# 47 matmuls of a zero tile ahead of the first product of a joint-classifier kernel

## The chip, the cores and the metric

The kernel runs on one NeuronCore of a Trainium2 chip. The metric is the device time of one execution in microseconds (us). The engines are TensorE (PE, with its weight loads as PEld), VectorE (DVE), ScalarE (ACT), GpSimd (POOL) and SyncE (SP), each with its own instruction stream; they meet at semaphores.

## The reference

Each of 512 rows has 64 logits, four variables of 16. Four softmaxes are joined by outer products to 65,536 values a row. The labels sum them to class counts, these are divided by the sum over rows, and the ratios are applied to the same joint values.

```python
splits = np.cumsum((16, 16, 16, 16))[:-1]
variables = [jax.nn.softmax(p, axis=-1) for p in jnp.split(logits, splits, axis=-1)]
joint = variables[0]
for v in variables[1:]:
    joint = jnp.einsum('b...,ba->b...a', joint, v)
flat = joint.reshape(B, -1)                              # 512 x 65536
num_y_joint = jnp.einsum('bj,by->yj', flat, y_true)      # y_true is 512 x 100
num_joint = jnp.sum(flat, axis=0)
prob_y_joint = jnp.clip(jnp.maximum(num_y_joint, 1e-6) / jnp.maximum(num_joint, 1e-6), 0.0, 1.0)
probs = jnp.einsum('yj,bj->by', prob_y_joint, flat)
```

## The kernel before

The joint value is split in two factors. `p` is (variable 1) x (variable 2) x (variable 3), cut into 32 tiles of 128 joint indices by 512 rows; `q` is (variable 0) x (labels and a column of ones), in four groups of four values of variable 0, 4 x 101 = 404 columns each. The 512 rows lie as 128 partitions by KC = 4 chunks. Products need more than fp16, so p and q are split in high and low fp16 parts, and each product is three matmuls: high by high, high by low, low by high.

There are 4 groups x 32 tiles = 128 steps. A step has a *count* on TensorE (12 matmuls of 404 columns into a PSUM bank `numbers0` to `numbers3`, lines 366 to 373), a *ratio* on VectorE (five instructions, `make_ratios`, lines 276 to 293), and a *join* on TensorE (12 matmuls of 400 columns into `joined0` to `joined3`, lines 384 to 390). TensorE runs four counts ahead of the joins, one bank a slot; joins also need the transposed p (`pt_hi`, `pt_lo`), which SyncE makes by DMA transposes from `p_hi` and `p_lo` in the first group. After a group's last join ScalarE copies the joined banks out, and GpSimd folds them into `acc`; for the last group VectorE does this itself, in 16 adds (line 354), before the store.

The order is written out by hand, engine by engine, with semaphores. The start is this. SyncE loads the logits. VectorE subtracts the maximum, ScalarE takes exp, VectorE makes `v1s`, the first half of `p23` (line 235, semaphore `p23_made`), the sums and `v0n` (line 304, `v0n_made`), the first half of `qf` (line 243), the second half of `p23` and of `qf`. ScalarE makes `p_hi` of tile 0 (four activations, line 187), the first half of `q_hi` (line 195), `p_hi` of tile 1, the second half of `q_hi`, and then `p_hi` of tiles 2 and 3, four activations of 128x256 together, and so on in a loop. VectorE makes `q_lo` (line 249) and `p_lo` (line 270) behind them.

TensorE does nothing until p_hi's tile 0 and q_hi's first half are there. Its first four counts are split up by hand so that each matmul stands as early as its operands come (lines 404 to 435): two products of tile 0 and two of tile 1 with the first half of `q_hi`, four with the second half, four with the first half of `q_lo`, then, behind a wait for `p_hi_made` 4, eight products of tiles 2 and 3, then four more with `q_lo` and the `p_lo` products. From then on joins and counts alternate.

GpSimd's only work at the start is the memset of the ones column of `labels` and of `acc`. `SLOTS` is 4, `LANES` 128.

Of the kernel before, what the change touches and what calls it, by code (L numbers as in the profile page):

```python
# [25 lines left out]
FP16 = mybir.dt.float16  # L26
# [5 lines left out]
def joint_classifier(nc: bass.Bass, logits: bass.AP, y_true: bass.AP, probs: bass.AP):  # L32
    ROWS, WIDTH = logits.shape
    CLASSES = y_true.shape[1]
    LANES = 128
# [20 lines left out]
    with ctx:  # L56
        def sb(name, shape, dt):
            return ctx.enter_context(nc.sbuf_tensor(name, shape, dt))

        def pb(name, shape, dt):  # L60
            return ctx.enter_context(nc.psum_tensor(name, shape, dt))

        def sem(name):
            return ctx.enter_context(nc.semaphore(name))

        SLOTS = 4
        TURN_SEMS = 4

        x = sb("x", [LANES, KC * NV, S], FP32)
# [3 lines left out]
        v0f = sb("v0f", [LANES, KC, S], FP32)  # L73
        v1s = sb("v1s", [LANES, KC, S], FP32)
        labels = sb("labels", [LANES, KC, CW], FP32)
        p23 = sb("p23", [LANES, KC, 2 * HALF], FP32)

        p_hi = sb("p_hi", [LANES, TILES * TW], FP16)
# [6 lines left out]

        den = sb("den", [LANES, SLOTS, AG], FP32)
        inv = sb("inv", [LANES, SLOTS, AG], FP32)
        ratio = sb("ratio", [LANES, SLOTS, PW], FP32)
        r_hi = sb("r_hi", [LANES, SLOTS, PW], FP16)
        r_lo = sb("r_lo", [LANES, SLOTS, PW], FP16)  # L90

# [3 lines left out]

        numbers = [pb(f"numbers{i}", [LANES, 512], FP32) for i in range(SLOTS)]
        joined = [pb(f"joined{i}", [LANES, 512], FP32) for i in range(KC)]
# [6 lines left out]
        shifted = sem("shifted")  # L104
        exps = sem("exps")
        v1s_made = sem("v1s_made")
        v0n_made = sem("v0n_made")
        p23_made = sem("p23_made")
        q_made = sem("q_made")
# [4 lines left out]
        p_ready = sem("p_ready")  # L114
        pt_landed = [sem(f"pt_landed{j}") for j in range(TURN_SEMS)]
        numbers_ready = sem("numbers_ready")
# [16 lines left out]
        @block.sync  # L133
        def _(sp):
            sp.dma_start(x[:, :, :], logits.rearrange("(p k) (v s) -> p (k v) s", k=KC, s=S)).then_inc(logits_in, 16)

            def turn(out, src, i):
                return sp.dma_start_transpose(
                    out[:, i * 2 * TW:(i + 1) * 2 * TW].rearrange("p (c b) -> p c b", b=LANES),
                    src[:, i * 2 * TW:(i + 1) * 2 * TW])  # L140

            for i in range(S):
                landed = pt_landed[i % TURN_SEMS]
                if i >= TURN_SEMS:
                    sp.wait_ge(landed, i // TURN_SEMS * 32)
                sp.wait_ge(p_hi_made, 2 * i + 2)
                turn(pt_hi, p_hi, i).then_inc(landed, 16)
                sp.wait_ge(p_ready, 2 * i + 2)
                turn(pt_lo, p_lo, i).then_inc(landed, 16)
            sp.wait_ge(added, KC * AG)  # L150
            sp.dma_start(probs.rearrange("(p k) y -> p k y", k=KC), acc[:, :, :]).then_inc(stored, 16)
            sp.wait_ge(stored, 16)

        @block.gpsimd
        def _(pool):
            pool.memset(labels[:, :, CLASSES:CW], 1.0).then_inc(ones_set, 1)
            pool.memset(acc[:, :, :], 0.0).then_inc(acc_set, 1)
            pool.wait_ge(p_ready, TILES)
            pool.tensor_scalar(v0f[:, :, :], v0n[:, :, :], 1.0 / UP ** 3, None, ALU.mult).then_inc(v0f_made, 1)
            pool.wait_ge(v0f_made, 1)  # L160
            pool.wait_ge(acc_set, 1)
            with pool.Fori(1, GROUPS) as g:
                pool.wait_ge(left_made, g * KC)
                pool.tensor_tensor(part[:, :, :, :], left[:, :, :, :],  # L164
                                   v0f[:, :, bass.ds((g - 1) * AG, AG)].unsqueeze(3).broadcast_to([LANES, KC, AG, CLASSES]),
                                   ALU.mult).then_inc(sum_chain, 1)
                pool.wait_ge(sum_chain, 3 * g - 2)
                pool.tensor_tensor(part[:, :, 0:2, :], part[:, :, 0:2, :], part[:, :, 2:4, :],
                                   ALU.add).then_inc(sum_chain, 1)
                pool.wait_ge(sum_chain, 3 * g - 1)  # L170
                pool.tensor_tensor(part[:, :, 0, :], part[:, :, 0, :], part[:, :, 1, :], ALU.add).then_inc(sum_chain, 1)
                pool.wait_ge(sum_chain, 3 * g)
                pool.tensor_tensor(acc[:, :, :], acc[:, :, :], part[:, :, 0, :], ALU.add).then_inc(summed, 1)

                pool.wait_ge(summed, g)
# [183 lines left out]
        def _(pe):  # L359
# [24 lines left out]
            def join(g, tile, slot, first=False, final=False):  # L384

                pe.wait_ge(ratios_ready, g * TILES + tile + 1)
                for k in range(KC):
                    if first and g:
                        pe.wait_ge(left_made, (g - 1) * KC + (k + 1))
                    join_chunk(tile, slot, k, first, final)  # L390
# [7 lines left out]
            def first_lo_hi(tile):  # L398
# [2 lines left out]
                                     start=False, stop=(k == KC - 1))  # L401
                last.then_inc(numbers_ready, 1)

            pe.wait_ge(p_hi_made, 1)
            pe.wait_ge(q_hi_made, 1)
            for k in range(KC // 2):
# [30 lines left out]
            for tile in range(TILES - SLOTS):  # L437
                if tile % 2 == 0:
                    pe.wait_ge(pt_landed[tile // 2 % TURN_SEMS], (tile // 2 // TURN_SEMS + 1) * 32)
                join(0, tile, tile % SLOTS, first=(tile == 0))  # L440
# [4 lines left out]
            for g in range(GROUPS):  # L445
# [8 lines left out]
                if g < GROUPS - 1:  # L454
                    pe.wait_ge(q_ready, 2 + (g + 1) * KC)
                    for j in range(SLOTS):
                        tile = TILES - SLOTS + j
                        if g == 0 and j % 2 == 0:
                            pe.wait_ge(pt_landed[tile // 2 % TURN_SEMS], (tile // 2 // TURN_SEMS + 1) * 32)
                        join(g, tile, j, final=(j == SLOTS - 1))  # L460
# [33 lines left out]
```

## Time and profile before

| | us |
|---|---|
| Median of 3 runs | 540.55 |
| Lowest and highest of them | 540.05, 541.52 |
| The profiled execution | 540.03 |
| Its span, first to last instruction | 537.8 |
| PE busy | 524.5 (98%) |
| DVE busy | 294.3 (55%) |
| ACT busy | 41.5 (8%) |
| First matmul starts | 8.24 |

The rows below come from the profiled execution. Times are microseconds from the start of its span. In a timeline row the first number is the start and the second the duration, and square brackets tell how long the engine was idle before and which instruction released it. A matmul's duration reaches over the start of the next one, as matmuls are pipelined; the pace of TensorE is the distance between two starts. PEclk is the granted TensorE clock as a share of 2.4 GHz as the profiler recorded it.

### The profile page before, as it was taken

To read this page: it belongs to the slowest core of one execution; us is meant where nothing else is said; L and a number is where in the kernel's file an instruction comes from. 1 tells how busy PE (TensorE), PEld (TensorE's weight loads), DVE (VectorE), ACT (ScalarE), POOL (GpSimd) and SP (SyncE) were. 2 spreads that over 40 slices of the span, in tenths; PEclk is the share of its full clock that TensorE was granted. 3 is DMA by queue.
4 is the path that set the end of the run, shared out by engine and by line. 5 is a ranking of instruction groups with operands and counts; after the bars stand their busy time and mean duration, and the time that the engine had idled before them with its cause. 6 is when DMAs were issued, how large, how long until landed. Compare 5 with 4: busy or idle time off the path is not lost.

```text
span 537.8 us, 8613 instructions
## 1 busy us (share of the span) xinstructions
PE 524.5 (98%) x3072; PEld 299.5 (56%) x3072; DVE 294.3 (55%) x757; ACT 41.5 (8%) x96; POOL 22.5 (4%) x19
## 2 busy tenths in 40 slices
PE   3999999999999999999999999999999999999996
PEld 1555555555555555555555555555555555555553
DVE  7887667654575444444467444444446444444445
ACT  6950000000110000000020000000001000000000
POOL 0000000000050000000022000000005000000000
PEclk9999999999999999999999999999999999999999
DMA  1744243340000000000000000000000000000000
GB/s 45 141 95 66 53 78 60 59 60 1 0 1 1 1 0 0 0 0 0 0 1 1 0 0 0 1 0 0 0 0 1 0 1 0 0 0 0 0 0 15
DMA packets 34624, 9.17 MB, mean 17 GB/s; under 512 B 34352, under 2 KB 34608, under 8 KB 34608
## 3 DMA queue, kind: packets, MB, share of 16 engines
q1 hardware_dynamic: 34080, 8.73, 8.8%
q8 instruction: 13, 0.21, 0.2%
q10 hardware_dynamic: 528, 0.20, 0.1%
q14 instruction: 3, 0.02, 0.0%
HBM read 0.34 MB, written 0.20 MB: 1 GB/s over the span
## 4 chain that ended last, share of the span: by engine, by line
PE 97%; DVE 2%; ACT 0%; DMA 0%; issue 0%; ACTq 0%; DVEq 0%
PE joined L378 16%; PE joined L379 16%; PE joined L380 16%; PE numbers L370 16%; PE numbers L372 16%; PE numbers L371 16%; DVE acc L354 1%; PE numbers L393 1%; PE numbers L396 1%; PE numbers L400 1%; DMA x<-in_r_logits_dram 0%; ACT p_hi L187 0%; DVE qf L243 0%; ACT q_hi L195 0%; DVE p L235 0%
## 5 line engine op out<-in xcount | busy, mean ns | idle before, releaser
L379 PE MATMUL joined<-r_lo,pt_hi 128*128 128x400 f16 x512 | 170.4, 333 | 0.0
L380 PE MATMUL joined<-r_hi,pt_lo 128*128 128x400 f16 x512 | 170.4, 333 | 0.0
L378 PE MATMUL joined<-r_hi,pt_hi 128*128 128x400 f16 x512 | 170.3, 333 | 0.0
L370 PE MATMUL numbers<-q_hi,p_hi 128*128 128x404 f16 x496 | 166.5, 336 | 0.0
L372 PE MATMUL numbers<-q_hi,p_lo 128*128 128x404 f16 x496 | 165.5, 334 | 0.0
L371 PE MATMUL numbers<-q_lo,p_hi 128*128 128x404 f16 x496 | 165.4, 333 | 0.0
L280 DVE TENSOR_SCALAR den<-numbers 128x4 f32<-128x4 f32 x128 | 20.7, 162 | 215.9 <-PE numbers L372 215.0
L292 DVE SCALAR_TENSOR_TENSOR r_lo<-ratio,r_hi 128x400 f16<-128x400 f32 x128 | 78.4, 612 | 4.4
L285 DVE SCALAR_TENSOR_TENSOR ratio<-numbers,inv 128x400 f32<-128x400 f32 x128 | 73.5, 574 | 4.4
L379 PEld LDWEIGHTS joined<-r_lo,pt_hi 128*128 (+1 forms) x512 | 50.0, 98 | 36.9
L378 PEld LDWEIGHTS joined<-r_hi,pt_hi 128*128 (+1 forms) x512 | 49.8, 97 | 37.0
L380 PEld LDWEIGHTS joined<-r_hi,pt_lo 128*128 (+1 forms) x512 | 50.0, 98 | 36.6
L371 PEld LDWEIGHTS numbers<-q_lo,p_hi 128*128 (+1 forms) x496 | 48.7, 98 | 36.2
L372 PEld LDWEIGHTS numbers<-q_hi,p_lo 128*128 (+1 forms) x496 | 48.0, 97 | 36.9
L370 PEld LDWEIGHTS numbers<-q_hi,p_hi 128*128 (+1 forms) x496 | 48.3, 97 | 36.1
L290 DVE TENSOR_SCALAR r_hi<-ratio 128x400 f16<-128x400 f32 x128 | 48.9, 382 | 4.4
L221 ACT ACTIVATE left<-joined 128x400 f32<-128x400 f32 x12 | 5.9, 503 | 317.8 <-PE joined L380 317.7
L187 ACT ACTIVATE p_hi<-p,v1s 128x256 f32 (+1 forms) x68 | 26.6, 480 | 0.9 <-DVE p L235 0.9
L270 DVE SCALAR_TENSOR_TENSOR p_lo<-p,v1s,p_hi 128x256 f16<-128x256 f32 x64 | 26.6, 480 | 0.0
L283 DVE RECIPROCAL inv<-den 128x4 f32<-128x4 f32 x128 | 22.8, 178 | 4.4
L164 POOL TENSOR_TENSOR part<-left,v0f 128x1600 f32<-128x1600 f32 x3 | 8.6, 2862 | 277.7 <-ACT left L221 277.7
L393 PE MATMUL numbers<-q_hi,p_hi 128*128 128x404 f16 x16 | 4.7, 432 | 8.5 <-ACT q_hi L195 8.2
(31 smaller groups left out, 62.5 us busy)
## 6 DMA issues: line engine op xcount, KB each, us to landing
pt_hi<-p_hi SPq DMA_TRANSPOSE x16, 3.1
pt_lo<-p_lo SPq DMA_TRANSPOSE x16, 3.2
labels<-in_r_y_true_dram ACTq DMA_DIRECT2D x1, 200.0 KB, 2.8
out_dram<-acc SPq DMA_DIRECT2D x1, 200.0 KB, 1.9
x<-in_r_logits_dram SPq DMA_DIRECT2D x1, 128.0 KB, 2.2
```

What stands on the lines that cost most here:

```text
L187: last = act.activation(o[:, h0:h1, k, :], p23[:, k, h0 * HALF:h1 * HALF].rearrange("p (h n) -> p h n", n=HALF), ACT.Copy, scale=v1s[:, k, ...
L270: last = dve.scalar_tensor_tensor(lo[:, :, k, :], p23[:, k, :].rearrange("p (h n) -> p h n", n=HALF), v1s[:, k, bass.ds(i, 1)], hi[:, :, k ...
L283: dve.reciprocal(inv[:, slot, :], den[:, slot, :]).then_inc(inv_made, 1)
L285: dve.scalar_tensor_tensor(ratio[:, slot, :].rearrange("p (a y) -> p a y", a=AG), got[:, :, 0:CLASSES], STABLE, inv[:, slot, :].unsqueeze( ...
L290: dve.tensor_scalar(r_hi[:, slot, :], ratio[:, slot, :], UP, 0.0, ALU.min, ALU.max).then_inc(r_hi_made, 1)
L292: dve.scalar_tensor_tensor(r_lo[:, slot, :], ratio[:, slot, :], UP, r_hi[:, slot, :], ALU.min, ALU.subtract).then_inc(ratios_ready, 1)
L370: pe.matmul(out, p_at(p_hi, tile, k), q_at(q_hi, g, k), start=(k == 0), stop=False)
L371: pe.matmul(out, p_at(p_hi, tile, k), q_at(q_lo, g, k), start=False, stop=False)
L372: last = pe.matmul(out, p_at(p_lo, tile, k), q_at(q_hi, g, k), start=False, stop=(k == KC - 1))
L378: pe.matmul(out, p_at(pt_hi, tile, k), r_hi[:, slot, :], start=first, stop=False)
L379: pe.matmul(out, p_at(pt_hi, tile, k), r_lo[:, slot, :], start=False, stop=False)
L380: last = pe.matmul(out, p_at(pt_lo, tile, k), r_hi[:, slot, :], start=False, stop=final)
```

## The change

A tile `idle` of 128x256 fp16 is set to zero by GpSimd, ahead of its two other memsets. On TensorE, ahead of the first product, 47 matmuls are written out: the weights are the tile's first 128 columns, the moving operand all 256 of them, the output 256 columns of the PSUM bank `numbers0`. That bank is later started anew by the first product (`start=True`), so that nothing of the zeros is left. 22 of the 47 wait for the zero tile, nine for the first half of `p23`, and 16 for `v0n`. All else, the products' order and waits included, is as before; only line numbers move (393 is 398 in the changed kernel, 396 is 401).

```diff
+        IDLE_W = 256
+        IDLE_START, IDLE_EXPS, IDLE_V0 = 22, 9, 16
...
+        idle = sb("idle", [LANES, IDLE_W], FP16)
...
+        idle_set = sem("idle_set")
...
         def _(pool):
+            pool.memset(idle[:, :], 0.0).then_inc(idle_set, 1)
             pool.memset(labels[:, :, CLASSES:CW], 1.0).then_inc(ones_set, 1)
...
+            def idle_turns(n):
+                for _ in range(n):
+                    pe.matmul(numbers[0][:, 0:IDLE_W], idle[:, 0:LANES], idle[:, :], start=True, stop=True)
+
+            pe.wait_ge(idle_set, 1)
+            idle_turns(IDLE_START)
+            pe.wait_ge(p23_made, 1)
+            idle_turns(IDLE_EXPS)
+            pe.wait_ge(v0n_made, 1)
+            idle_turns(IDLE_V0)
+
             pe.wait_ge(p_hi_made, 1)
             pe.wait_ge(q_hi_made, 1)
```

TensorE's stream begins like this before the change (the first row is the block's entry):

```order
L358 UNCONDITIONAL_BRANCH [waits barrier_Pool_Activation_PE_DVE_SP_release]
L393 MATMUL numbers<-q_hi,p_hi 128x404 [waits q_hi_made,p_hi_made]
L393 MATMUL numbers<-q_hi,p_hi 128x404
L393 MATMUL numbers<-q_hi,p_hi 128x404 [waits p_hi_made]
L393 MATMUL numbers<-q_hi,p_hi 128x404
L393 MATMUL numbers<-q_hi,p_hi 128x404 [waits q_hi_made]
L393 MATMUL numbers<-q_hi,p_hi 128x404 x3
L396 MATMUL numbers<-q_lo,p_hi 128x404 [waits q_ready]
```

And like this after it:

```order
L363 UNCONDITIONAL_BRANCH [waits barrier_Pool_Activation_PE_DVE_SP_release]
L411 MATMUL numbers<-idle 128x256 [waits idle_set]
L411 MATMUL numbers<-idle 128x256 x21
L411 MATMUL numbers<-idle 128x256 [waits p23_made]
L411 MATMUL numbers<-idle 128x256 x8
L411 MATMUL numbers<-idle 128x256 [waits v0n_made]
L411 MATMUL numbers<-idle 128x256 x15
L398 MATMUL numbers<-q_hi,p_hi 128x404 [waits q_hi_made,p_hi_made]
L398 MATMUL numbers<-q_hi,p_hi 128x404
```

The first product now stands behind 47 matmuls and three more waits; from it on the rows are the same.

GpSimd's stream at the entry of its block, before:

```order
L154 UNCONDITIONAL_BRANCH [waits barrier_Pool_Activation_PE_DVE_SP_gather]
L156 MEMSET labels 128x4
L157 MEMSET acc 128x400
L159 ISA
L159 TENSOR_SCALAR v0f<-v0n 128x64 [waits p_ready]
```

and after:

```order
L158 UNCONDITIONAL_BRANCH [waits barrier_Pool_Activation_PE_DVE_SP_gather]
L160 MEMSET idle 128x256
L161 MEMSET labels 128x4
L162 MEMSET acc 128x400
L164 ISA
L164 TENSOR_SCALAR v0f<-v0n 128x64 [waits p_ready]
```

The zero tile's memset has gone in front of the two others, and nothing else has moved.

## Rows read from the trace of the kernel before

**Rows 1.** The page: busy time (share of the span), and the chain that ended last by engine.
```profile
PE 524.5 (98%) x3072; PEld 299.5 (56%) x3072; DVE 294.3 (55%) x757; ACT 41.5 (8%) x96; POOL 22.5 (4%) x19
PE 97%; DVE 2%; ACT 0%; DMA 0%; issue 0%; ACTq 0%; DVEq 0%
```

**Rows 2.** Windows, all engines: length, busy us (xinstructions), PEclk, DMA share, GB/s.
```profile
12.19:530.00 517.81, 517.81 (x3045) 296.65 (x3044) 281.27 (x726) 33.50 (x79) 21.88 (x13) 1.00 0.09 16
```

**Rows 3.** Timeline of PE, one row a matmul: start us, us, engine, line, operation [idle].
```profile
8.24 0.49 PE L393 MATMUL numbers<-q_hi,p_hi 128*128 128x404 f16 x1 [8.24 <-ACT q_hi L195]
9.31 0.52 PE L393 MATMUL numbers<-q_hi,p_hi 128*128 128x404 f16 x1 [0.25 <-ACT p_hi L187]
10.08 0.52 PE L393 MATMUL numbers<-q_hi,p_hi 128*128 128x404 f16 x1
10.39 0.54 PE L393 MATMUL numbers<-q_hi,p_hi 128*128 128x404 f16 x1
11.06 0.54 PE L393 MATMUL numbers<-q_hi,p_hi 128*128 128x404 f16 x1
11.40 0.44 PE L396 MATMUL numbers<-q_lo,p_hi 128*128 128x404 f16 x1
11.68 0.51 PE L396 MATMUL numbers<-q_lo,p_hi 128*128 128x404 f16 x2
12.02 0.34 PE L396 MATMUL numbers<-q_lo,p_hi 128*128 128x404 f16 x1
12.19 0.33 PE L393 MATMUL numbers<-q_hi,p_hi 128*128 128x404 f16 x1
```

**Rows 4.** Timeline of PE and its weight loads at the first join.
```profile
18.38 0.33 PE L378 MATMUL joined<-r_hi,pt_hi 128*128 128x400 f16 x1
18.38 0.10 PEld L379 LDWEIGHTS joined<-r_lo,pt_hi 128*128 128x128 f16 x1
18.54 0.33 PE L379 MATMUL joined<-r_lo,pt_hi 128*128 128x400 f16 x1
```

**Rows 5.** Windows of PE's first products and of the end; PE's last matmul in the timeline.
```profile
8.24:11.40 3.16, 2.91 (x8) 1.00 0.28 56
...
537.00:537.70 0.70, 0.00 (x0) 0.00 (x0) 0.00 (x0) 0.00 (x0) 0.00 (x0) 0.68 0.00 0
...
532.69 0.33 PE L380 MATMUL joined<-r_hi,pt_lo 128*128 128x400 f16 x1
```

**Rows 6.** Timeline of ACT: q_hi's second half and the last p_hi of tiles 2, 3.
```profile
9.17 0.86 ACT L195 ACTIVATE q_hi<-qf 128x808 f16<-128x808 f32 x1
11.13 0.49 ACT L187 ACTIVATE p_hi<-p,v1s 128x256 f32 x1
```

**Rows 7.** Timeline of DVE and SP to the first join; the page's transposes (median us to landing).
```profile
10.06 1.00 DVE L249 TENSOR_TENSOR q_lo<-qf,q_hi 128x808 f16<-128x808 f32 x1 [0.45 <-ACT q_hi L195]
13.74 0.48 DVE L270 SCALAR_TENSOR_TENSOR p_lo<-p,v1s,p_hi 128x256 f16<-128x256 f32 x1
15.14 0.16 DVE L280 TENSOR_SCALAR den<-numbers 128x4 f32<-128x4 f32 x1 [0.91 <-PE numbers L400]
16.56 0.58 DVE L292 SCALAR_TENSOR_TENSOR r_lo<-ratio,r_hi 128x400 f16<-128x400 f32 x1
12.67 1.23 SPq L138 DMA_TRANSPOSE pt_lo<-p_lo  x1
...
pt_lo<-p_lo SPq DMA_TRANSPOSE x16, 3.2
```

**Rows 8.** Timeline of POOL at the start.
```profile
0.71 0.10 POOL L156 MEMSET labels<- 128x4 f32 x1 [0.29 <-POOLq L482]
0.75 0.43 POOL L157 MEMSET acc<- 128x400 f32 x1
```

**Rows 9.** Timeline of DVE: the first half of p23 (p) and v0n.
```profile
4.38 0.68 DVE L235 TENSOR_TENSOR p<-x 128x512 f32<-128x512 f32 x1
5.92 0.23 DVE L304 SCALAR_TENSOR_TENSOR v0n<-x,whole 128x64 f32<-128x64 f32 x1
```

## The prediction

> **What bounds the kernel now.** I read the busy shares first: PE is busy 98% of a span of 537.8 us, and the chain that ended last is 97% PE [rows 1]. Then the windows: from 12.19 to 530.00 us PE is busy 517.81 of 517.81 us [rows 2], so whatever time PE gains or loses by 12.19 us is carried to its last matmul, and to the 16 adds on VectorE and the store behind it, which wait for that. What is before 12.19 us decides this change, since nothing behind it is edited.
>
> There the PE timeline, one matmul a row, has to be read by start-to-start distance [rows 3]. Products of 404 columns that wait for nothing start at 10.39, at 11.06 (the next but one) and at 11.40 us, 0.34 us a product: 404 columns in 0.337 us are 1.2 GHz. From 12.02 to 12.19 it is 0.17 us, which is 2.4 GHz, and it stays so (18.38 and 18.54 us, [rows 4]). The one after 11.40 starts at 11.68, an intermediate distance, so the clock rose near 11.6 us, about 3.4 us after the first matmul at 8.24. The granted-clock column prints 1.00 for 8.24 to 11.40 as well [rows 5]; it contradicts the distances, and I go by the distances. It does print the fall: 0.68 in 537.00 to 537.70, while the last matmul starts at 532.69 and lasts 0.33 [rows 5]. So PE kept the full clock through at least 3.9 us of idleness.
>
> **What a full clock at the first product is worth.** I walk PE's waits with 0.17 us a product. Products 1 and 2 start at 8.24, as before, for q_hi's first half. Products 3 and 4 wait for p_hi and start at 9.31. The next four wait for q_hi's second half (ACT 9.17 + 0.86 = 10.03) and start at 10.08 [rows 3, 6]; four products end their turn at 10.08 + 0.68 = 10.76, and four with q_lo at 11.44. Now PE meets a wait that the low clock had hidden: the eight products of tiles 2 and 3 wait for p_hi_made 4, the last of four activations, 11.13 + 0.49 = 11.62 [rows 6]. With the 0.05 us that stood between ACT's end and PE's start at 10.08, they start at 11.67 instead of 12.19. **Gain: 0.52 us.** The ten or so products at the low clock take 10 x 0.167 = 1.7 us more than at the full one, but most of that lies in PE's waits for ScalarE.
>
> What is late next? The products of q_lo's second half need 10.06 + 1.00 = 11.06; they would start at 13.04. The p_lo products of tiles 0 and 1 would start at 13.73 and need their p_lo, for which SyncE's transpose waits too; it is issued at 12.67. Those of tiles 2 and 3 would start at 16.48 and need 13.74 + 0.48 = 14.22 themselves. The first join would start at 18.38 - 0.52 = 17.86; the ratios it needs end at 16.56 + 0.58 = 17.14 and follow PE earlier, since VectorE stood idle 0.91 us before den (from 14.22 it could start), and that transpose, which the join needs, lands 3.2 us later, 15.9 [rows 7]. Nothing takes the 0.52 us back.
>
> **The idle matmuls, part by part.** *Start.* GpSimd's first memset in the block stands at 0.71, and 128x400 of fp32 takes 0.43 us [rows 8]; a 128x256 fp16 tile lies between 0.10 and 0.43, I take 0.3. So PE starts near 1.05 us (bounds 0.85 to 1.2). The labels' and acc's memsets move back by as much; the ones are first read behind v0n, at 6.15 us [rows 9], so this costs nothing. *One matmul.* No row has 256 columns with 128 rows of fp16; scaled from the rows it is 256/404 of 0.337 = 0.213 us at 1.2 GHz and of 0.170 = 0.108 us at 2.4 GHz. Its weight load takes 0.10 us and runs beside the matmul before it [rows 4], so the lower bound is 0.108 and the upper, if the load hides nothing, 0.21; the hidden load is what every row shows. *Clock.* If it rises 3.4 us after the first matmul, as before, that is at 4.4 us. Then 16 matmuls run low, six high, and batch one ends near 5.1; p23 is there at 4.38 + 0.68 = 5.06 [rows 9]. Batch two ends near 6.05, v0n comes at 5.92 + 0.23 = 6.15, and batch three, 16 x 0.108 = 1.7 us, ends at 7.9, before the first product's 8.24. The two small holes are far below the 3.9 us idleness that kept the clock up [rows 5].
>
> *If it rises later*, more of the 47 run low and the last ends later. With a rise at 8.0 us, 33 run low until 8.1, and the last ends at 8.1 + 14 x 0.108 = 9.6; the twelve products behind it, full speed, 2.04 us, then end at 11.65, just where ScalarE lets PE on anyway. So the gain of 0.52 us is whole for every rise up to 8.0 us, and it is used up (idle matmuls ending at 10.15, since 12.19 - 2.04 = 10.15) only by a rise near 9.1, some 8 us after the first matmul. Everything else on PE, in particular order and waits, stands as it was.
>
> **Span and medians.** The profiled execution took 540.03 us (span 537.8 and 2.2 around it). 540.03 - 0.52 = 539.51. Its time lies 0.52 under the median of 540.55, and the three timed runs spread over 1.47 us. A rise that comes later in some executions explains such a spread well, as each us of dense products at half clock costs up to half a us: 1.47 us would be 2.9 us later. If so, the changed kernel, whose clock may rise as late as 8.0 us without a loss (4.4 + 2.9 = 7.3), sheds this spread too, and its median is near 539.5. If the spread has another source (the input's DMA ahead of all work, for one), it stays, and the median is 540.55 - 0.52 = 540.03. The Trainium skill, TensorE: Matmul & The Clock Gate, section "What's actually happening", says that the point of the rise varies from run to run of one kernel. The one trace here can't show that; by the trace alone 540.03 would stand, by the page 539.5. I take 539.6, nearer the first, since the profiled run coincides with the fastest of the three, as it would if the rise had its earliest place there.
>
> **Rivals.**
> 1. *Spread stays*: gain only against the same execution, 540.0 us. For it: a clock record of one execution proves nothing on others. Against: a low clock is the only part of this kernel seen here that changes within an execution.
> 2. *Gain does not come*: the zero matmuls take longer than their columns, or the clock rises after 9.1 us. With 16 at the low clock until 4.4 us, the other 31 may take (10.15 - 4.4) / 31 = 0.185 us each before the gain is gone. If the 0.10 us load hid nowhere, they would take 0.31 us low and 0.21 high: 11 by 4.4 us, 36 more until 11.9, the twelve products until 13.9, which is 1.7 us late. That spans 540.0 to 542.3, and I give the middle of partly hidden loads, 540.3 to 540.9. Against: the load hides in every 0.17 us, and 0.098 still fits in 0.108.
> 3. *Slower*: matmuls of zeros do not raise the clock. All 47 at 0.213 take 10.0 us and end at 11.1; the first product moves from 8.24 to 11.1 and the clock rises 3.4 us later, at 14.5. Ten products at 0.337 and two at 0.17 end at 14.8 against 12.19: +2.6 us, 542.7 on the profiled execution, 543.2 on the median. It decides from an idle end of 10.15 on. For it: no row shows the clock with zero data. Against: both clock levels here stood with the same kind of data, so nothing ties the clock to data rather than to matmuls issued.
> 4. *The change does more*: over 1.6 us gained would need early waits on ScalarE or VectorE to go as well; none is touched.
>
> **How the numbers follow.** Clock up in time and spread shed (539.5): 0.50. Clock up, spread kept (540.0): 0.32. No gain (540.3 to 540.9): 0.11. Slower (542.7): 0.04. Faster than all this: 0.03, of which 0.02 beyond 0.3%. I predict 539.6; the range is 539.1 to 540.8: 0.4 under the likeliest case for what PE and DMA starts vary, and up over most of the no-gain case. 0.3% is 1.6 us, about what a measurement of this kernel can tell from no change: faster is under 538.9, slower over 542.2. That gives faster 0.02, same 0.94, slower 0.04.
>
> **What would show it.** In the profile after: idle matmuls start near 1.05 us at 0.21 us and change to 0.11 before 8.0 us; the last ends by 8.24 to 9.6; the first product is followed by the second 0.17 us later; the eight products of tiles 2 and 3 start at 11.67, released by ACT's p_hi; the first join at 17.86; span 537.3. Wrong, if products still stand 0.33 us apart, if the first product starts after 9.6, or if the eight products start near 12.19 or later; and the spread of the timed runs tells between rival 1 and the forecast: shed, it is under 0.7 us.

## The result, and the profile after

| | before | after |
|---|---|---|
| Median of 14 runs, us | 540.6 | 539.47 |
| Lowest and highest, us | 540.05, 541.52 | 539.37, 539.55 |
| Ratio of the mean times, 95% interval | | 0.9977 (0.9969 to 0.9985) |
| Profiled execution, us | 540.03 | 539.47 |
| Its span, us | 537.8 | 537.2 |

The change takes 1.1 us or 0.21% off the median, and the distance from the lowest to the highest run goes from 1.47 to 0.18 us. The profiled execution shows 0.6 us of it; the rest is that the execution profiled before was one of the fastest of its kernel.

The page of the kernel after, its busy shares and the chain by engine, which answers to [rows 1]:

```profile
PE 531.1 (99%) x3119; PEld 305.4 (57%) x3119; DVE 294.3 (55%) x757; ACT 41.5 (8%) x96; POOL 22.8 (4%) x20
PE 96%; DVE 2%; ACT 1%; DMA 0%; issue 0%; ACTq 0%; DVEq 0%
```

PE has 47 matmuls more (3119 against 3072) and 6.6 us more busy time in a span that is 0.6 us shorter. The time at stake is in the first 12 us. This is the timeline of PE there (start us, us, engine, line, operation, how many; in brackets the idle time before and its releaser), to be laid beside [rows 3]; lines 393, 396 and 400 of before are 398, 401 and 405 here:

```profile
1.08 7.94 PE L411 MATMUL numbers<-idle 128*128 128x256 f16 x47 [1.08 <-POOL idle L160]
8.86 0.90 PE L398 MATMUL numbers<-q_hi,p_hi 128*128 128x404 f16 x4
10.01 0.86 PE L398 MATMUL numbers<-q_hi,p_hi 128*128 128x404 f16 x4 [0.25 <-ACT q_hi L200]
10.71 0.85 PE L401 MATMUL numbers<-q_lo,p_hi 128*128 128x404 f16 x4
11.61 1.55 PE L398 MATMUL numbers<-q_hi,p_hi 128*128 128x404 f16 x8
12.99 0.85 PE L401 MATMUL numbers<-q_lo,p_hi 128*128 128x404 f16 x4
13.68 1.54 PE L405 MATMUL numbers<-q_hi,p_lo 128*128 128x404 f16 x8
...
17.81 0.33 PE L383 MATMUL joined<-r_hi,pt_hi 128*128 128x400 f16 x1
```

The idle matmuls run from 1.08 us to the first product at 8.86. The first four products stand 0.17 to 0.21 us apart, the next four start at 10.01 behind ScalarE, and the eight of tiles 2 and 3 start at 11.61, where they stood at 12.19. The first join is at 17.81 (18.38 before). The last matmul starts at 532.12 (532.69 before), and the distance from first join to last matmul is 514.31 us in both, so what is gained at the start arrives whole at the end. From 11.61 to 530 us PE has no idle time (window of PE: length, busy us, matmuls, PEclk, DMA share, GB/s):

```profile
11.61:530.00 518.39, 518.39 (x3047) 1.00 0.09 16
```

The pace of the idle matmuls is read from windows of PE: length, busy us, (matmuls that touch the window), PEclk, DMA share, GB/s. The clock column stays at 1.00 here as it did in [rows 5]:

```profile
5.00:6.00 1.00, 1.00 (x7) 1.00 0.00 0
6.00:6.50 0.50, 0.50 (x4) 1.00 0.00 0
6.50:7.00 0.50, 0.50 (x6) 1.00 0.00 0
7.00:8.00 1.00, 1.00 (x12) 1.00 0.00 0
```

Seven matmuls touch the us from 5 to 6, twelve the one from 7 to 8. The matmuls overlap, so these counts are two or so above the number of starts, but the change of pace lies near 6.5 us: 5.4 us after the first matmul, at 1.08, and before the first product.

What releases the two later groups of products is in ScalarE's timeline, which answers to [rows 6]:

```profile
9.09 0.86 ACT L200 ACTIVATE q_hi<-qf 128x808 f16<-128x808 f32 x1
```

```profile
11.06 0.49 ACT L192 ACTIVATE p_hi<-p,v1s 128x256 f32 x1
```

q_hi's second half ends at 9.95 and PE goes on at 10.01; the last p_hi of tile 3 ends at 11.55 and PE goes on at 11.61. In this execution the logits landed 0.08 us earlier than in the one before: VectorE's first reduce starts at 2.83 (2.91 before). Of the 0.58 us between 12.19 and 11.61, then, 0.08 are the input's and 0.50 the change's.

### The profile page after: what moved, and what is told of

Same layout as the page of the kernel before. It is cut to its first block, busy times and chain, and to the rows that moved or that the text cites. A ratio compares the mean times of both kernels' runs of the same rounds, so it can differ in the third digit from the quotient of the medians.

```text
span 537.2 us, 8708 instructions
## 1 busy us (share of the span) xinstructions
PE 531.1 (99%) x3119; PEld 305.4 (57%) x3119; DVE 294.3 (55%) x757; ACT 41.5 (8%) x96; POOL 22.8 (4%) x20
## 4 chain that ended last, share of the span: by engine, by line
PE 96%; DVE 2%; ACT 1%; DMA 0%; issue 0%; ACTq 0%; DVEq 0%
PE joined L383 16%; PE joined L385 16%; PE joined L384 16%; PE numbers L375 16%; PE numbers L376 16%; PE numbers L377 16%; DVE acc L359 1%; PE numbers L405 1%; DMA x<-in_r_logits_dram 0%; PE numbers L401 0%; ACT p_hi L192 0%; PE numbers L398 0%; ACT q_hi L200 0%; DVE qf L248 0%; DVE p L240 0%
## 5 line engine op out<-in xcount | busy, mean ns | idle before, releaser
L375 PE MATMUL numbers<-q_hi,p_hi 128*128 128x404 f16 x496 | 166.1, 335 | 0.0
L248 DVE TENSOR_TENSOR qf<-v0n,labels 128x404 f32<-128x404 f32 (+1 forms) x14 | 10.5, 753 | 0.0
```

What stands on the lines that cost most here:

```text
L375: pe.matmul(out, p_at(p_hi, tile, k), q_at(q_hi, g, k), start=(k == 0), stop=False)
```

## The experiments

All numbers are medians of 5 to 14 runs, with the lowest and the highest, in us. Each set had runs of the kernel before on the same chip beside it; their medians were 540.6 to 540.8, and they went from 539.74 to 541.52. A ratio is that of the mean times, to the kernel before of the same set.

| | idle matmuls | order of products | median | lowest, highest |
|---|---|---|---|---|
| the kernel before | none | as before | 540.6 | 540.05, 541.52 |
| the change | 22, 9, 16 | as before | 539.47 | 539.37, 539.55 |
| e1_one_each | 1, 1, 1 | as before | 540.67 | 540.27, 541.25 |
| e2_start_only | 22, 0, 0 | as before | 540.66 | 539.99, 541.47 |
| e3_ones | 22, 9, 16, of ones | as before | 539.46 | 539.37, 539.54 |
| e4_plus16 | 22, 9, 32 | as before | 539.63 | 539.39, 540.74 |
| e6_third_batch_only | 0, 0, 16 | as before | 539.86 | 539.38, 540.57 |
| e12_third_batch_4 | 22, 9, 4 | as before | 539.45 | 539.39, 539.56 |
| e13_no_third_batch | 22, 9, 0 | as before | 539.46 | 539.39, 540.87 |
| e7_order_no_idle | none | both edits | 540.81 | 540.05, 541.18 |
| e10_swap_and_idle | 22, 9, 16 | first edit | 539.46 | 539.40, 539.56 |
| e9_chunks_and_idle | 22, 9, 16 | second edit | 539.15 | 538.95, 539.21 |
| e8_order_and_idle | 22, 9, 16 | both edits | 538.58 | 538.41, 538.72 |
| e11_both_12 | 22, 9, 12 | both edits | 538.62 | 538.59, 538.73 |

### Is it the matmuls, or what comes with them? (e1_one_each)

```diff
-        IDLE_START, IDLE_EXPS, IDLE_V0 = 22, 9, 16
+        IDLE_START, IDLE_EXPS, IDLE_V0 = 1, 1, 1
```

> One zero matmul in each of the three batches instead of 22, 9 and 16; the tile, its memset and the three waits stay. Theory (the gain is the clock, raised by the 47): the gain and the narrow spread both go, median 540.4 to 540.8 us, spread of the runs over 1 us, products 0.34 us apart until 11 us or later. Rival (the gain comes from the layout, the memset, the waits or from TensorE's instructions being fetched early): 539.5 us with a spread of 0.2 us, as with the change.

Measured: 540.67 us, 540.27 to 541.25, ratio to before 1.0001 (0.9992 to 1.001). The gain is gone, and the narrow spread too, though at 0.98 us the spread stayed just under the 1 us that I had expected. The tile, its memset, the three waits and an early first matmul on PE are all still there. Its PE timeline:

```profile
1.08 0.39 PE L411 MATMUL numbers<-idle 128*128 128x256 f16 x1 [1.08 <-POOL idle L160]
5.08 0.39 PE L411 MATMUL numbers<-idle 128*128 128x256 f16 x1 [3.60 <-DVE p L240]
6.16 0.39 PE L411 MATMUL numbers<-idle 128*128 128x256 f16 x1 [0.69 <-DVE v0n L309]
8.19 0.83 PE L398 MATMUL numbers<-q_hi,p_hi 128*128 128x404 f16 x2 [1.64 <-ACT q_hi L200]
9.27 2.29 PE L398 MATMUL numbers<-q_hi,p_hi 128*128 128x404 f16 x6 [0.25 <-ACT p_hi L192]
11.36 1.55 PE L401 MATMUL numbers<-q_lo,p_hi 128*128 128x404 f16 x4
12.70 1.49 PE L398 MATMUL numbers<-q_hi,p_hi 128*128 128x404 f16 x7
```

From 11.36 to 12.70 there are four products, 0.335 us each: the low clock holds until almost 13 us, later than in [rows 3]. The rival (layout, memset, waits, instructions fetched early) falls.

### Do zeros count less? (e3_ones)

```diff
-            pool.memset(idle[:, :], 0.0).then_inc(idle_set, 1)
+            pool.memset(idle[:, :], 1.0).then_inc(idle_set, 1)
```

> The idle tile is 1.0 instead of 0. Theory (the clock follows matmuls issued, not their data): 539.5 us, spread 0.2. Rival (data matters, zeros raise the clock later): the idle matmuls end earlier than 8.9 us in the trace, time 539.4 or less; or, if it matters the other way, over 540.

Measured: 539.46 us, 539.37 to 539.54, the same as with zeros. Its idle matmuls end earlier, as this row of its PE timeline tells (7.94 us in the kernel after):

```profile
1.08 6.93 PE L411 MATMUL numbers<-idle 128*128 128x256 f16 x47 [1.08 <-POOL idle L160]
```

That alone does not say that ones raise the clock sooner. With zeros, the profiles of e8 and e9 below have their 47 from 1.08 us for 7.31 and 7.37 us, and in e10, with zeros as well, the distance between two starts changes from 0.21 to 0.11 us at 3.8 us, ahead of the 4.0 us of this run with ones. Its first 22 are done after 3.87 us (at the low clock all the way they took 4.87 us, in e2 below):

```profile
1.08 3.87 PE L411 MATMUL numbers<-idle 128*128 128x256 f16 x22 [1.08 <-POOL idle L160]
```

The times are the same within 0.01 us, and no run here shows a part that the data plays.

### How much may the idle matmuls overrun? (e4_plus16)

```diff
-        IDLE_START, IDLE_EXPS, IDLE_V0 = 22, 9, 16
+        IDLE_START, IDLE_EXPS, IDLE_V0 = 22, 9, 32
```

> 22, 9 and 32: 16 idle matmuls more, 1.73 us at full clock. Theory (an idle end up to 9.6 us is free, after that each us costs one): the idle matmuls end at 9.5 us if the clock rises at 4.4, at 10.7 if at 6.4 as in the profile of the change, at 11.1 if at 7.8; so 539.5 to 541.1 us, median 540.4, and a spread near 1 us is back. Rival (no slack, all 1.73 us is lost): 541.2 us with spread 0.2. Rival (TensorE's idle matmuls are hidden anyway): 539.5 us.

Measured: 539.63 us. Eight of the 11 runs are within 539.39 and 539.73, three at 540.13, 540.53 and 540.74. The shape is the one that the theory gives, a floor at 539.5 and a tail of over a us, and both rivals fall: 16 more matmuls are neither free nor a fixed 1.73 us. The median is 0.8 us under what I expected, since I took the profile of the change, with its rise at 6.5 us, for a typical one; it is the latest rise in any profile here whose matmuls start at 1.08 us and run on. The profiled execution of this kernel shows the other case:

```profile
1.08 8.76 PE L411 MATMUL numbers<-idle 128*128 128x256 f16 x63 [1.08 <-POOL idle L160]
9.67 1.54 PE L398 MATMUL numbers<-q_hi,p_hi 128*128 128x404 f16 x8
11.05 0.85 PE L401 MATMUL numbers<-q_lo,p_hi 128*128 128x404 f16 x4
11.74 1.53 PE L398 MATMUL numbers<-q_hi,p_hi 128*128 128x404 f16 x8
```

The first product follows the 63 idle matmuls at 9.67, so the clock was up early, and the twelve products run without a hole to 11.74, 0.13 us later than the 11.61 of the change. Its time is 539.57, 0.10 more than 539.47. That is the slack of the prediction, an end of the idle matmuls near 9.6 us, met to within 0.1.

### Which of the three batches does it take? (e2, e6, e12, e13)

e2_start_only sets `22, 0, 0`, e6_third_batch_only `0, 0, 16`, e12_third_batch_4 `22, 9, 4` and e13_no_third_batch `22, 9, 0` on the same line.

> Only the first batch of 22; they end near 5.8 us if the clock is still low, and TensorE is idle until the first product near 8.2 us. Theory (the rise comes at a point that differs from run to run, and 2.4 us of idleness don't lose it, as 3.9 us did not at the end of the kernel before): where it rises before 5.8 us 539.5 us, where it doesn't, up to 541; median near 539.9, spread over 0.5 us. Rival (the second and third batch do nothing): 539.5 us in all runs, spread under 0.2. Rival (idleness of 2.4 us loses the clock): 540.5 us, as before the change.

Measured: 540.66 us, 539.99 to 541.47; nothing is left of the gain. I had expected half of it. Here the profiler recorded the clock's fall. Windows of PE, columns as above:

```profile
5.00:6.00 1.00, 0.96 (x5) 1.00 0.00 0
6.00:7.00 1.00, 0.00 (x0) 1.00 0.00 0
...
8.00:9.00 1.00, 0.51 (x2) 1.00 0.00 0
9.00:10.00 1.00, 0.52 (x2) 0.85 0.00 0
10.00:11.00 1.00, 0.92 (x3) 0.50 0.47 94
...
12.00:13.00 1.00, 1.00 (x4) 0.50 0.00 0
13.00:14.00 1.00, 1.00 (x7) 0.94 0.12 25
```

The 22 idle matmuls end at 5.95. PE is then idle for 2.27 us, and the four products up to 10 us fill only 1.03 us. The clock had been up: the first two products start 0.17 us apart, at 8.23 and 8.40. It is at 0.85 between 9 and 10 us, at 0.50 until 13, and back at 0.94 between 13 and 14. So PE spent the whole dense stretch from 10.08 to 13.1 us at 1.2 GHz, the very stretch that the clock was wanted for. The timed runs say that it was not this execution alone. Behind each stands the mean granted clock of its span: 0.991 to 0.997 in all 11 runs of e2, against 0.998 to 1.0 in 88 of the 89 runs of the kernel before that stood beside the experiments.

The hole was 2.27 us. My argument from the end of the kernel before, where nearly 4 us of idleness did not lower the clock, took one execution for a rule, and the ends of the other kernels contradict it. In e9 PE is idle from 532.28 us on and the clock falls between 534.3 and 534.5, after 2.0 to 2.2 us; in e2 itself PE is idle from 533.77 and the clock is still up when the span ends, 4.7 us later. Here are PE's last matmul and the windows of PE behind it, for e9 and then for e2:

```profile
531.95 0.33 PE L389 MATMUL joined<-r_hi,pt_lo 128*128 128x400 f16 x1
533.00:534.30 1.30, 0.00 (x0) 1.00 0.00 0
534.50:535.50 1.00, 0.00 (x0) 0.50 0.00 0
```

```profile
533.44 0.33 PE L385 MATMUL joined<-r_hi,pt_lo 128*128 128x400 f16 x1
537.00:538.50 1.50, 0.00 (x0) 1.00 0.37 137
```

> The changed kernel with 22, 9 and 4 idle matmuls: they end near 6.6 us when the clock rises early, and TensorE is idle up to 1.6 us before the first product (2.27 us with the first batch alone). Theory (the clock falls when TensorE has been idle for most of a stretch, holes between the first products included): part of the runs lose the clock, median 539.8 us, spread over 0.8. Rival (only a single hole over 2 us matters): 539.5 us with a spread of 0.2.

Measured: 539.45 us, 539.39 to 539.56. My theory said that some runs would lose the clock; none of 9 did, and the rival's number stands (its rule, that only a single hole over 2 us matters, is not shown by that). The profiled execution has its idle matmuls until 7.64 and a hole of 0.59 us.

> The changed kernel with 22 and 9 idle matmuls and no third batch: in its two neighbours 35 matmuls kept 539.45 us in all runs and 22 lost the gain. The hole ahead of the first product is 1 to 2.2 us by the place of the rise. Theory (what decides is whether matmuls fill enough of the time until the first product, so there is a middle): part of the runs lose the clock, median 539.6 us, highest run over 540.3. Rival (the third batch has no part in the gain): 539.5 us, spread 0.2. Rival (without it the gain is lost in most runs, as with 22): median over 540.3 us.

Measured: 539.46 us, but 539.39 to 540.87: 11 of 12 runs are under 539.56, and one is at 540.87, as before the change. That run has a mean granted clock of 0.997, the other 11 have 0.998 to 1.0. The theory's middle is there, if 1 run of 12 is enough to say so. In the profiled one, at 539.41, the idle matmuls end at 6.14 and PE is idle for 1.95 us without losing the clock:

```profile
1.08 5.06 PE L411 MATMUL numbers<-idle 128*128 128x256 f16 x31 [1.08 <-POOL idle L160]
8.10 0.50 PE L398 MATMUL numbers<-q_hi,p_hi 128*128 128x404 f16 x2 [1.95 <-ACT q_hi L200]
9.18 0.52 PE L398 MATMUL numbers<-q_hi,p_hi 128*128 128x404 f16 x2 [0.58 <-ACT p_hi L192]
9.95 0.86 PE L398 MATMUL numbers<-q_hi,p_hi 128*128 128x404 f16 x4 [0.25 <-ACT q_hi L200]
```

Thus with 22 matmuls the runs are spread as before, 31 lose the gain in one run of 12, and 35 (9 runs) and 47 (14 runs) in none; so few runs do not tell 31 from 35. The difference between a hole of 1.95 us (kept) and one of 2.27 us (lost) is small, and by the ends above no single length decides: idleness lowered the clock after some 2.1 us in one execution and not within 4.7 us in another. By which rule it falls is open; these runs do not tell the length of a hole from the amount of work ahead of it.

> Only the third batch: 16 idle matmuls behind v0n, from 6.1 us, at the low clock until 9.5 us. Theory (the time at which matmuls begin sets when the clock can rise): the earliest rise is 9.5 us, which gives 539.5 us; three us later gives 541.0; median 540.0 to 540.4, spread over 1 us. Rival (the 16 matmuls right ahead of the products are what counts): 539.5 us, spread 0.2.

Measured: 539.86 us, 539.38 to 540.57, a little better than expected, with the spread of over a us that the theory asks for. The idle matmuls start at 6.28 and the low clock reaches into the products:

```profile
6.28 3.57 PE L411 MATMUL numbers<-idle 128*128 128x256 f16 x16 [6.28 <-DVE v0n L309]
9.64 2.42 PE L398 MATMUL numbers<-q_hi,p_hi 128*128 128x404 f16 x8
11.90 0.85 PE L401 MATMUL numbers<-q_lo,p_hi 128*128 128x404 f16 x4
12.59 1.53 PE L398 MATMUL numbers<-q_hi,p_hi 128*128 128x404 f16 x8
```

Its eight products of tiles 2 and 3 start at 12.59 and its time is 540.43. What the change adds to this is the start five us earlier; with it every one of the 14 runs has the gain. The early start by itself does not do it, as e2 shows.

### What bounds the start now, and a faster kernel (e7 to e11)

With the clock up, PE waits for ScalarE at 10.01 and at 11.61. Two edits of PE's order fill these waits. The first (the swap) puts q_lo's four products ahead of those with q_hi's second half:

```diff
+            pe.wait_ge(q_ready, 1)
+            for tile in range(2):
+                for k in range(KC // 2):
+                    first_hi_lo(tile, k)
             pe.wait_ge(q_hi_made, 2)
             for tile in range(2):
                 for k in range(KC // 2, KC):
                     first_hi_hi(tile, k)
-            pe.wait_ge(q_ready, 1)
-            for tile in range(2):
-                for k in range(KC // 2):
-                    first_hi_lo(tile, k)
```

The second (chunks) lets PE take the eight products of tiles 2 and 3 in pairs, as soon as ScalarE has a chunk of p_hi:

```diff
+                    if parts and k < KC - 1:
+                        last.then_inc(p_hi_parts, 1)
...
-            with act.Fori(1, S) as i:
+            make_p_hi(1, 0, 2, parts=True)
+            with act.Fori(2, S) as i:
...
-            pe.wait_ge(p_hi_made, 4)
-            for tile in range(2, 4):
-                for k in range(KC):
-                    first_hi_hi(tile, k)
+            for k in range(KC):
+                if k < KC - 1:
+                    pe.wait_ge(p_hi_parts, k + 1)
+                else:
+                    pe.wait_ge(p_hi_made, 4)
+                for tile in range(2, 4):
+                    first_hi_hi(tile, k)
```

> No idle matmuls. Two edits of the order in the kernel before: TensorE does the four q_lo products of tiles 0 and 1 (first half) ahead of the four with q_hi's second half, and takes the eight products of tiles 2 and 3 chunk by chunk, each pair as soon as ScalarE has that chunk's p_hi. Theory (at the low clock TensorE itself is late, so ScalarE's order hides nothing): 540.5 us, at most 0.1 us better than before, spread over 1 us. Rival (TensorE's waits for ScalarE cost their time at either clock): 540.0 us.

> Only the first of the two edits of the order (q_lo's four products ahead of those with q_hi's second half), with the 47 idle matmuls. Theory (the twelve products then end at 11.0 us but the eight wait for all of ScalarE's p_hi until 11.6 all the same): 539.5 us, nothing gained by itself, though it is worth 0.6 us together with the other edit. Rival (each edit is worth its own share): 539.1 us.

> Only the second of the two edits (chunk by chunk), with the 47 idle matmuls. Theory: the twelve products end at 11.4 us instead of waiting until 11.6, so 0.2 us is gained: 539.25 us. Rival (the wait for p_hi of tiles 2 and 3 is no bound): 539.5 us.

> The same two edits of the order, with the 47 idle matmuls. Theory (with the clock up, ScalarE's p_hi of tiles 2 and 3 is what TensorE waits for): the twelve products end at 11.0 us, the eight end at 12.4 instead of 13.0: 538.9 us. Rival (the start is bounded elsewhere, such as the idle matmuls' end or the first ratio): 539.5 us.

> Both edits of the order with 22, 9 and 12 idle matmuls, four fewer. Theory (four fewer end 0.4 us earlier at full clock, which only executions with a late rise need, and the hole before the first product stays under 1 us, which loses nothing): 538.5 us, spread 0.3, as with 16. Rival (a hole of 0.8 us more ahead of the products loses the clock): 539 to 540 us with a spread over 1 us.

Measured, against 540.6 to 540.8 before and 539.47 with the change: both edits without idle matmuls 540.81 (ratio 1.0, 0.9991 to 1.0009, with 540.82 for the kernel before on that chip); the swap alone with them 539.46; the chunks alone 539.15; both 538.58; both with four matmuls fewer 538.62. The first equals the kernel before of its chip, as its theory had it; e10, e9 and e11 lie within 0.12 us of theirs, and e8 is 0.3 us under its 538.9. So the two edits are worth nothing at the low clock, and at the full clock 0.0 and 0.3 us singly and 0.9 together. The swap only lets PE be earlier at a wait that ScalarE ends; PE's timeline of e10 has it:

```profile
9.70 0.85 PE L401 MATMUL numbers<-q_lo,p_hi 128*128 128x404 f16 x4
10.39 0.85 PE L398 MATMUL numbers<-q_hi,p_hi 128*128 128x404 f16 x4
11.71 1.55 PE L398 MATMUL numbers<-q_hi,p_hi 128*128 128x404 f16 x8 [0.47 <-ACT p_hi L192]
```

Everything ahead is done 0.47 us before p_hi comes. With both edits this wait is gone (PE's timeline of e8; the 0.47 us in its first row are an earlier wait, for p_hi of tile 1):

```profile
9.20 0.52 PE L402 MATMUL numbers<-q_hi,p_hi 128*128 128x404 f16 x2 [0.47 <-ACT p_hi L193]
9.56 0.85 PE L405 MATMUL numbers<-q_lo,p_hi 128*128 128x404 f16 x4
10.25 2.22 PE L402 MATMUL numbers<-q_hi,p_hi 128*128 128x404 f16 x12
12.30 0.85 PE L405 MATMUL numbers<-q_lo,p_hi 128*128 128x404 f16 x4
```

Twelve products run from 10.25 to 12.30 without a hole, and the four after them start 0.69 us earlier than in the kernel after (12.99). The first join is at 17.12 against 17.81, again 0.69. The span is 536.5 against 537.2. The medians differ by 0.89, and some 0.2 us of that lie outside the span: the timed runs of e8 have 2.05 us around it, those of the kernel after 2.26. The chip is not the reason, as e6 has 2.27 on the chip of e8, and e11 has 2.11 on that of e10, which has 2.28. All four kernels with the second edit have 2.05 to 2.15 us there, and all others 2.25 to 2.28. So this part comes with the second edit; why is open. Of the 0.3 us of e9, 0.1 is of this kind. The ratio of e8 to before is 0.9957 (0.9943 to 0.9971); it is the best kernel here, and e11, whose interval overlaps it, does as well with 43 idle matmuls.

e7 shows the other side. Windows of PE, without idle matmuls:

```profile
13.00:14.00 1.00, 1.00 (x5) 1.00 0.18 38
...
15.00:16.00 1.00, 1.00 (x7) 1.00 0.95 188
```

Five matmuls touch the us from 13 to 14, seven the one from 15 to 16. The clock was low until past 14 us (two starts are 0.34 us apart until 14.28, 0.17 from 14.49 on), 6.2 us after the first matmul at 8.18, and the time of this execution is 541.18.

## Why the prediction was right

**What bounds the kernel.** Confirmed: from 11.61 to 530 us PE has no idle time, and the 514.31 us from first join to last matmul are the same in every kernel compared. Time won ahead of 12 us is won at the end.

**The 0.52 us.** Confirmed, with 0.50 in the profile. The wait that the low clock had hidden, p_hi of tiles 2 and 3, ends last, as worked out, and e8 and e9 showed it by taking it away. The first join was forecast at 17.86 and came at 17.81, of which 0.08 are the earlier input. None of the later waits took anything back.

**The spread is shed.** This was the choice between 539.5 and 540.0, and the runs decide for the first. The median gained 1.1 us, twice what the profile of before allowed, and the spread fell from 1.47 to 0.18 us. That a late rise makes a run longer is shown by e1 (rise near 13 us, 540.67) and e7 (past 14 us, 541.18), beside the 11.6 us and 540.03 of the execution profiled before. These are three kernels, one execution of each. For the timed runs of one kernel there is the mean granted clock of each. Of the 89 runs of the kernel before that stood beside the experiments, 27 took over 541.1 us, and 26 of these have 0.997 or 0.998; of the other 62 only one (541.04 us) is that low. In the traces of all kernels but e2 the only recorded fall is the one behind the last matmul, and a low clock ahead of the first recorded change counts as full. So this mean tells where the clock's fall at the end lay and not how the start went; but as it goes with the time, the longest runs are tied to the clock's course. The 14 runs of the changed kernel have 0.998 to 1.0 too, and their time no longer follows it: 539.37 and 539.55 us both stand at 0.998. That some tenths of the spread before have another source is not excluded. The prediction was also wrong to see the earliest possible rise in the execution profiled before: later runs of that kernel went down to 539.74 us.

The Trainium skill, TensorE: Matmul & The Clock Gate, section "What's actually happening", has the rise at a point that differs from run to run, by 500 ns to either side. That it differs agrees with this case; the size does not. Here the rise came 3.4 us after the first matmul in the profile before, 5.4 in the one after and 6.2 in e7's, and the measurement decides. It is the reason that the median gained 0.6 us more than one trace of before could show.

**The idle matmuls.** They start at 1.08 us (forecast 1.05, memset 0.31 us) and keep the pace of their columns, 0.213 and 0.109 us from start to start, so their weight loads hide, and rival 2 falls. The size that was off is the place of the rise. I put it at 4.4 us, as if the delay of one execution were fixed; in the profile it was near 6.5, and the first product followed the idle matmuls at 8.86, where they should have been done at 7.9. That the number held all the same is no luck: the prediction had worked out a slack up to 9.6 us for a later rise, which took it, and e4 measured that slack.

**The step that was wrong** is the evidence for holes. The prediction took the idleness at the end of the kernel before, at least 3.9 us at full clock, for the length that the clock survives. e2 lost the clock with a hole of 2.27 us between 22 idle matmuls and the first products, and e9 lost it some 2.1 us after its last matmul. The changed kernel has no such hole, so the number was not hurt, and this was luck as far as the argument goes; a change with batches a little further apart would have been forecast wrong by the same argument.

**Rivals 3 and 4.** Zeros do raise the clock, and ones do no better. Nothing else got faster, and the change stayed inside the 0.3% on either side: the median fell by 0.21%, the mean by 0.23%.

## What to carry to other kernels

Where a kernel's first dense matmuls are paced by a clock that is still low, matmuls on a spare tile from the earliest moment on buy back both the median and the spread, as long as they end so early that the work behind them is still in time for the last wait that another engine decides (here an end at 9.6 us for p_hi at 11.6); work that slack out first, because the place of the rise moves by microseconds and the overrun with it. Do not leave holes of 2 us or more between them and the real work: one of 2.27 us lost the whole gain here. Then walk the waits again at full speed: edits of the order that were worth nothing before (540.81 with them, 540.8 without) were worth 0.9 us afterwards as a pair (538.58 against 539.47), and 0.0 and 0.3 us one by one.

## What the runs showed of the hardware

- In the twelve profiles whose matmuls run on from the first, the clock rose 2.7 (e10) to 6.2 us (e7) after the first matmul; it was 3.4 in the one before and 5.4 in the one after. The 89 runs of the kernel before lie between 539.74 and 541.47 us, and those over 541.1 show a mean granted clock of 0.997 or 0.998, all but one.
- It fell near 9.7 us in e2, with PE idle from 5.95 to 8.23 us and busy 1.03 us between 8 and 10, and came back near 13.1, 3 us after dense matmuls began at 10.08. Behind the last matmul of a kernel, with PE completely idle, it fell after some 2.1 us in e9, stayed up for nearly 4 us in the kernel before and for 4.7 us in e2.
- The granted-clock column prints 1.00 for a low clock ahead of the first recorded change (5 to 6 us in the kernel after, 8.24 to 11.40 in the one before). Only start distances tell there.
- Idle matmuls of zeros and of ones gave the same time, 539.47 and 539.46 us, and both raised the clock.
